# The up layer's second product in two row halves, in a decoder layer on one core

## What is computed

```python
def kmoe(x_flat, W_router, A, B, scale, bias, d_in1, d_in2, d_out1, d_out2, top_k):
    logits = x_flat @ W_router.T
    vals, idx = jax.lax.top_k(logits, top_k)
    probs = jax.nn.softmax(vals, axis=-1)
    xs = x_flat.reshape(-1, d_in1, d_in2)
    Y = jnp.einsum('nkoi,nij,nkpj->nkop', A[idx], xs, B[idx])
    out = jnp.einsum('nkop,nk->nop', Y, probs).reshape(-1, d_out1 * d_out2)
    return out * scale + bias
...
x_flat = x.reshape(-1, 32 * 32)
h = kmoe(x_flat, W_up, A_up, B_up, scale_up, bias_up, 32, 32, 64, 64, 2)
h = jax.nn.gelu(h, approximate=False)
y = kmoe(h, W_down, A_down, B_down, scale_down, bias_down, 64, 64, 32, 32, 2)
```

## Time and profile before

| | us |
|---|---|
| median of three runs | 2138.79 |
| fastest, slowest run | 2125.09, 2139.24 |
| span of the profiled execution | 2129.4 |
| TensorE busy in it | 1763.4 (83%) |
| second product of the up layer, TensorE busy | 170.2 |
| VectorE, ScalarE, GpSimd busy | 975.1, 862.5, 669.1 |

### The profile page before, as it was taken

One profiled execution on the slowest core, in us unless ns is written; L12 is line 12 of the kernel. 1 busy time (PEld: TensorE's weight loads), 2 busy tenths in 40 slices (PEclk: granted clock), 3 DMA queues, 4 the chain that ended last, 5 costly groups with the idle time before them and its releaser, 6 DMA issues.

```text
span 2129.4 us, 54205 instructions
## 1 busy us (share of the span) xinstructions
PE 1763.4 (83%) x17202; PEld 1370.1 (64%) x17202; DVE 975.1 (46%) x3954; ACT 862.5 (41%) x2550; POOL 669.1 (31%) x2386
## 2 busy tenths in 40 slices
PE   6888889798897988879788897988979889797865
PEld 5666757576575665757567575766757657576644
DVE  2345354544535445354443545445354453544543
ACT  2444344343443444345343443434434344343422
POOL 3114242322423134242332423224231242323333
PEclk9998979798797988969899797987979879798977
DMA  7000000000000000000000000000000000000000
GB/s 229 11 6 6 12 1 7 12 7 13 6 2 12 7 12 6 8 7 7 12 6 13 1 7 12 6 13 1 7 12 6 13 6 2 12 2 7 2 6 7
DMA packets 18653, 28.05 MB, mean 13 GB/s; under 512 B 2194, under 2 KB 17171, under 8 KB 18067
## 3 DMA queue, kind: packets, MB, share of 16 engines
q1 hardware_dynamic: 18322, 23.98, 3.7%
HBM read 19.78 MB, written 4.19 MB: 11 GB/s over the span
## 4 chain that ended last, share of the span: by engine, by line
PE 65%; issue 12%; DVE 9%; POOL 7%; POOLq 2%; ACT 2%; DVEq 0%; ACTq 0%
PE P L672 6%; PE G L800 6%; PE P L684 6%; PE G L838 5%; PE P L705 4%; PE X L749 4%; PE G L871 3%; POOL chosen_up L333 3%; PE PT L726 3%; PE P L657 3%; PE X L767 3%; PE PT L767 3%; PE X L752 3%; PE X L751 3%; PE F L824 3%
## 5 line engine op out<-in xcount | busy, mean ns | idle before, releaser
L346 POOL COPY chosen_dn<-experts 64x64 f32 x1024 | 197.1, 250 | 592.5 <-issue 513.1
L333 POOL COPY chosen_up<-experts 32x128 f32 x1024 | 285.6, 303 | 251.8 <-PE G L838 106.9
L970 DVE CUSTOM_DVE_ANT_0 probs<-S,distance 128x128 f32<-128x128 f32 (+1 forms) x512 | 153.5, 354 | 137.5 <-PE S L720 134.8
L557 ACT ACTIVATE probs<-probs,neg_max 128x128 f32<-128x128 f32 (+1 forms) x512 | 190.7, 443 | 41.0 <-DVE neg_max L970 39.7
L749 PE MATMUL X<-vals,probsT 128*128 128x65 f32 x512 | 109.6, 298 | 93.4 <-issue 47.7
L333 ACT COPY chosen_up<-experts 32x128 f32 x512 | 123.1, 292 | 132.8 <-PE G L838 122.7
L838 PE MATMUL G<-chosen_up,W 128*64 128x256 f32 x1024 | 170.2, 462 | 6.9 <-DVE W L1076 6.9
L749 PEld LDWEIGHTS X<-vals,probsT 128*128 128x128 f32 x512 | 83.2, 204 | 124.8 <-issue 123.7
L824 PE MATMUL F<-chosen_up,own 64*64 64x128 f32 x1024 | 98.1, 317 | 68.8 <-POOL chosen_up L333 66.3
L529 ACT ACTIVATE kT<-P,bk 128x256 f32<-128x256 f32 x128 | 53.7, 470 | 233.9 <-PE P L672 233.9
L672 PE MATMUL P<-ctxT,wk 128*128 128x256 f32 x512 | 144.8, 432 | 0.0
(11 more groups left out here) (129 smaller groups left out, 3313.6 us busy)
## 6 DMA issues: line engine op xcount, KB each, us to landing
x<-in_x SPq DMA_DIRECT2D x16, 256.0 KB, 2.6
ctxT<-in_ctxT SPq DMA_DIRECT2D x16, 256.0 KB, 2.6
out<-x2b SPq DMA_DIRECT2D x16, 256.0 KB, 2.9
r_dn<-in_r_dn SPq DMA_DIRECT2D x1, 2048.0 KB, 15.3
experts<-in_experts_up SPq DMA_DIRECT2D x2, 1024.0 KB, 22.0
wk<-in_xWk SPq DMA_DIRECT2D x1, 1024.0 KB
wo<-in_xWo SPq DMA_DIRECT2D x1, 1024.0 KB
wv<-in_xWv SPq DMA_DIRECT2D x1, 1024.0 KB, 7.6
```

What stands on the lines that cost most here:

```text
L333: last = copy(dst, src.rearrange("p (m c) -> p m c", m=2))
L346: last = copy(dst, src.rearrange("p (m c) -> p m c", m=2))
L557: act.activation(probs[e % 4][:, lo:hi], probs[e % 4][:, lo:hi], ACT.Exp, bias=neg_max[:, e % 4, rt:rt + 1], scale=-1.0).then_inc(probs_re ...
L970: dve.tensor_tensor_reduce(probs[e % 4][:, lo:hi], S[e % 2][:, lo:hi], distance[:, (1 - rt) * P:2 * P], SLOPES[e], TOP, ALU.add, ALU.min, ...
```

## The change

The second product is cut along its rows. Rows 0 to 63 hold the first two tokens of a group and rows 64 to 127 the other two, and each half of a block-diagonal matrix has only half of its columns filled. In the new kernel each half is a product of its own, over 64 rows and 128 moving columns: for each k there are four products (row half by group) where there were two. The upper half of the rows goes to bank F, the lower half to bank G, both in columns 256 to 383. The buffers `chosen_up` hold 128 columns for each k in place of 256. `pre` reads both banks in one instruction through a common tensor `FG` and writes the same 256 columns of `h`; the bias table is as wide as one half. Since F is now also read by `pre`, `first(v)` waits for `pre(v-1)` (`hidden_in`) in place of `weigh(v-1)`. `second` keeps its waits, with `hold` for one of them.

```diff
+        HALF = UP_TOK // 2 * F1
...
-        bias_up = sb("bias_up", [P, F1])
+        bias_up = sb("bias_up", [P, HALF])
...
-        A_UP, B_UP = TOPK * UP_TOK * F1, TOPK * F1
+        A_UP, B_UP = TOPK * HALF, TOPK * F1
...
+        FG = ctx.enter_context(nc.psum_tensor("FG", [P, 2, 512], F32))
+        F, G = FG[:, 0, :], FG[:, 1, :]
...
-                a, b = (k * UP_TOK + n) * F1, A_UP + k * F1
+                a, b = k * HALF + n % 2 * F1, A_UP + k * F1
...
-                    pe.wait_ge(W_ready, at(c, TURNS, v))
+                    pe.wait_ge(hidden_in, at(c, UP_PAIRS, v))
...
             def second(c, v):
                 pe.wait_ge(W_ready, at(c, TURNS, v + 1))
                 if v > 0:
-                    pe.wait_ge(hidden_in, at(c, UP_PAIRS, v))
+                    hold(pe, passed, hidden_in, at(c, UP_PAIRS, v))
                 else:
-                    pe.wait_ge(pm_ready, at(c, 6, 4))
-                n = UP_TOK * F1
+                    hold(pe, passed, pm_ready, at(c, 6, 4))
                 for k in range(TOPK):
-                    for j in (0, 1):
-                        w = j * B_UP + k * F1
-                        mm = pe.matmul(G[j * F1:(j + 1) * F1, 0:n], W[v % 2][:, w:w + F1],
-                                       chosen_up[(2 * v + j) % UP_SLOTS][:, k * n:(k + 1) * n], start=(k == 0), stop=(k == TOPK - 1))
+                    for half, to in enumerate((F, G)):
+                        rows = slice(half * F1, (half + 1) * F1)
+                        for j in (0, 1):
+                            w = j * B_UP + k * F1
+                            mm = pe.matmul(to[j * F1:(j + 1) * F1, 256:256 + HALF], W[v % 2][rows, w:w + F1],
+                                           chosen_up[(2 * v + j) % UP_SLOTS][rows, k * HALF:(k + 1) * HALF],
+                                           start=(k == 0), stop=(k == TOPK - 1))
                 mm.then_inc(second_done, 1)
...
-                dve.scalar_tensor_tensor(h[:, v * n:(v + 1) * n].rearrange("p (n o) -> p n o", o=F1),
-                                         G[:, 0:n].rearrange("p (n o) -> p n o", o=F1),
-                                         scale_up[:, 0:1], spread(bias_up[:, :], 1, UP_TOK),
+                dve.scalar_tensor_tensor(h[:, v * n:(v + 1) * n].rearrange("p (t w) -> p t w", t=2),
+                                         FG[:, :, 256:256 + HALF], scale_up[:, 0:1], spread(bias_up[:, :], 1, 2),
                                          ALU.mult, ALU.add).then_inc(hidden_in, 1)
...
-        "bias_up": np.tile(a["L0_ffn_bias_up"].reshape(F1, F1).T, (2, 1)),
+        "bias_up": np.tile(a["L0_ffn_bias_up"].reshape(F1, F1).T, (2, UP_TOK // 2)),
```

More of the change, by code:

```diff
@@ L249, in bank @@
             return ctx.enter_context(nc.psum_tensor(name, [P, 512], F32))
-        S0, S1, PT, X, P0, P1, F, G = (bank(n) for n in ("S0", "S1", "PT", "X", "P0", "P1", "F", "G"))
+        S0, S1, PT, X, P0, P1 = (bank(n) for n in ("S0", "S1", "PT", "X", "P0", "P1"))
+        FG = ctx.enter_context(nc.psum_tensor("FG", [P, 2, 512], F32))
+        F, G = FG[:, 0, :], FG[:, 1, :]
         S = [S0, S1]
```

## The result

The changed kernel takes 2165.61 us (median; 2162.05 to 2174.24), the kernel before, run beside it, 2139.01. The ratio is 1.0167, with an interval of 1.0111 to 1.0223: slower by 1.7%. The forecast was 2121, 0.8% faster, and the result lies above the range that went with it (2093 to 2152).

A forecast was written before the change was run, and what follows sets the result against it. TensorE, busy 83% of the span, was taken as the bound. Over fourteen batches, 21.8 us gained in odd turns less 4.2 for the moved wait gave span 2111.8; with 9.4 us up to the median, 2121 us (range 2093 to 2152).

The forecast's parts named there:

- an odd turn counts: Turns 1, 3, 5, 7: TensorE runs through, so a shorter second brings all behind it earlier, 0.39 us each (0.32 to 0.43).
- the price of the step: TensorE's slot for second: from 1.01 us to 0.62 (bounds 0.58 and 0.69), with four quarters of the array running together.
- The rival of the queue's order: In second: strict program order makes sixteen instructions nine steps, 1.12 us; 2149 us with the wait; chance 0.17.
- the four steps that the prediction set against it: Old second: strict order would need five steps, 1.14 us; the trace has 1.01, about four, so that order seemed not to hold.
- the moved wait in the body: Even turns: first(v+1) waits for pre(v), delaying pv; 0.05 + 0.20 + 0.05 = 0.3 us a batch (0.11 to 0.57).
- I price the odd turns at the high clock all the same: Odd turns: some 36 turns run low, but work pulled from the low stretch draws other work in, so 0.39 us each.
- the chance of the clock: Whole run: chance 0.19 that the granted clock takes the gain, 0.07 of it slower by over 1%.
- The rival of the clock: Behind turns 2 and 4: idle time brings low-clock spells of 1.7 us cost; 28 more give 2169 us; chance 0.19.
- the last two batches, at most 3.1 us of gain: Batches without all three stages: gain of at most 2 x 4 x 0.39 = 3.1 us, left to the range.
- the price of the wait over 14 batches alone: Moved wait counted only in the fourteen full batches: 14 x 0.3 = 4.2 us lost.
- that cover: Even turns of full batches: TensorE's idle time (1.26 and 0.78 us) covers first(v+1)'s wait and is just about used up.
- The range's upper end: 2152 us: strict queue order with the moved wait at its bound, 2138.8 + 6.2 + 8.0 = 2153, rounded in.

The follow-up runs named there:

- e8: Kernel before with four quarter products in odd turns only, plus unread products filling TensorE's idle time in six places of a batch: 2056.60 us, ratio 0.9634.
- e9: Kernel before with exactly the unread filling products of e8, and second unchanged: 2096.14 us, ratio 0.9814.
- e5: Changed kernel plus unread products in TensorE's idle time in turns 2, 4, 6 and ahead of pv of the sixth pair: 2103.59 us, ratio 0.9845.
- e2: Kernel before with the second expert's products left out of second; no moved wait, no 64 x 64 tiles: 2155.81 us, ratio 1.0107.
- e4: Kernel before with four quarter products in odd turns only; first waits for pre only behind an odd turn: 2148.58 us, ratio 1.0072.
- e10: e4 plus two unread products for each batch, ahead of pv of the sixth pair of heads: 2120.97 us, ratio 0.9942.
- e3: Changed kernel with the products of second done twice in even turns: 2147.62 us, ratio 1.0067.
- e1: Kernel before with the changed kernel's waits alone (first(v+1) waits for pre(v)); second keeps 256 columns: 2147.69 us, ratio 1.0079.
- e6: Kernel before plus unread products: two in turn 2, one in turn 4, two ahead of pv of the sixth pair: 2118.37 us, ratio 0.9930.

## Why the prediction was wrong, by its own steps

**Right: an odd turn counts.** From `second` to `score` in turn 7, where neither kernel is at the low clock, it took 3.92 us before (1105.94 to 1109.86 in the rows of before above) and takes 3.50 after (1515.10 to 1518.60), so this odd turn gives 0.42 where 0.39 was forecast; for all of them the 23.4 us between e8 and e9 are the nearest measure.

**Right: the price of the step.** The slot is 0.60 us (0.62 forecast, bounds 0.58 and 0.69). Four instructions start in one step. An instant of the timeline:

```profile
1487.49 0.34 PE L842 MATMUL FG<-chosen_up,W 64*64 64x128 f32 x4
```

Four are in flight at the start, where the earlier trace rows had two. The rival of the queue's order is thus out: nine steps would have taken 1.12 us. The Trainium skill, "TensorE: Matmul & The Clock Gate", Part 3 (packing small matmuls), says that matmuls keep strict program order at start and end. If the two instructions of a product stand side by side, as the prediction took it, the 0.60 us do not bear that out; but no row shows in which order they were issued, so the rule is neither confirmed nor refuted here, nor by the four steps that the prediction set against it.

**Right: the moved wait in the body.** From `second(4)` to `second(5)` it is 4.57 us (1501.91 to 1506.48) against 4.37 before (1092.53 to 1096.90), so 0.20, as forecast (0.11 to 0.35). Turn 2 is 0.09 longer in e5, at the high clock (1442.38 to 1447.33, 4.95, against 4.86 in the earlier trace rows). Turn 6 is 0.11 shorter (3.94 against 4.05), where 0.05 longer was forecast. Together 0.18 a batch instead of 0.3, read from one batch of each kernel.

**Wrong, and the step that failed: "I price the odd turns at the high clock all the same", and the chance of the clock.** By the steps so far a batch should be 4 x 0.41 - 0.18 = 1.5 us shorter. The thirteen batches were 17.1 us longer. The sentence on the earlier trace rows took the low stretches as given and let work only move into or out of them. They are not given: they are set off by how TensorE's work and idle time lie, and shortening the changed step altered where they stand and how long they last. e2 shows it with no other part of the change, e4 with odd turns alone, e5 and e10 in the other direction.

The sizes fit on the whole. Between 14 and 60 us behind `second(0)`, from turn 2 to past `pv` of the sixth pair, the low stretches of the traces add up, over the thirteen batches, to 45 us before, 113 in after, 107 in e2, 79 in e3, 86 in e4 and 0.1 in e5. An estimate takes half of the difference to before and the steps measured above: 0.41 us less for an odd turn (0.43 in e2, whose `second` takes 0.58) and 0.18 more a batch for the wait in after, e3 and e5. It gives the thirteen batches as 15 us longer in after (measured 17.1 longer), 2 shorter in e3 (3.4), 1 shorter in e4 (1.0) and 41 shorter in e5 (39.7). It is no exact price: in e1, e2, e6 and e10 it is off by 5 to 9 us, most in e2 (8 longer, measured 17.1). And low time elsewhere in the batch costs less, for there TensorE also waits: e8 has 68 us more of it than e9 and is shorter all the same.

The rival of the clock had the mechanism and nearly the size (28 more low stretches, 2169 us, against 2165.61). That it came so near is in part luck: it put them behind turns 2 and 4, where after has them behind turn 2 (in 11 of 14 batches, before in 8), behind turn 4 (3, before none) and at `pv` of the sixth pair (10, before 5), and it had nothing for the last two batches. It got a chance of 0.19, with a slow outcome at 0.07, because the rows showed idle time without a fall (0.78 us in turn 4) and the other direction seemed as open. What spoke for it was in the rows and was weighed too lightly: a fall directly behind idle time in the earlier trace rows, two batches 6.2 us apart with the same work, and a mean clock of 0.89 and 0.85 there, which is 22 and 30% of the time at the low level. In turns 2, 4 and 6 the change could only make the idle time longer, by the forecast's own reading, and a longer idle time had no way to a gain.

The Trainium skill, the same page, section "HAM oscillation", describes a loop in which waits between bursts of matmuls bring the clock down in each pass. After agrees in kind, with low stretches behind 1.70 and 1.42 us of idle time. The page's waits are for DMA and longer than these. That an idle time decides by itself is not borne out here: 1.42 us in before were followed by 1.00.

**Wrong: the last two batches, at most 3.1 us of gain, and the price of the wait over 14 batches alone.** I bounded this stage on the side of the gain only. Without attention and Fourier products between the turns, `first(v+1)` had been running under `pre(v)`, and that cover, which I named for even turns of the full batches, goes in every turn. In e1 the last two batches cost 18.6 us, in after, whose `second` is shorter, 11.7. In e2, with a short `second` and no moved wait, they cost 4.8; if after's clock costs as much, an estimate, some 7 of the 11.7 are the wait's. The range's upper end held 8.0 us for the wait, all of it in fourteen batches.

**The sum.** The forecast span was 2111.8, measured were 2163.9, 52.1 more. By parts: 33.4 in the thirteen batches (17.1 longer instead of 13 x 1.26 = 16.3 shorter), 6.0 in the fourteenth (4.7 instead of -1.3), 11.7 in the last two, 1.0 ahead. The first is what the low stretches cost by the estimate above (half of 113 less 45, 34). In the fourteenth batch the clock went from 0.88 to 0.83, and half of the low time that this adds is some 7 us, about the second. In the last two batches wait and clock are mixed. A small term was misread as well: the 9.4 us between span and median are no constant. After's profiled execution took 2165.65 us at a span of 2163.9, so 1.8 us lie around it, and if it is as much in before, the rest was that before's profiled execution was faster than the median one.

**Open.** Why the same idle time is followed by a fall in 12 of 14 batches of e4 and in 5 of 14 of before. A `second(7)` shorter by 0.41 us stands in front of it in e4, but before falls too at times with its long one. The runs show that the fall depends on more than the idle time just ahead of it, and that no fall came there where it was filled (e5, e6 and e10); what the chip goes by they do not show.

## What to carry to other kernels

Where TensorE's granted clock is below 1 for part of the span, cost a change by what it does to the idle time in front of and behind each TensorE step, not by the step alone: shortening work in front of a wait lengthens the wait, and here that turned a forecast gain of 0.8% into a loss of 1.7%. Before such a change is judged, fill the idle time with a few products that nobody reads, in both kernels; here that gave 1.9% without the change and 3.7% with the part of it that counts. And when a wait is moved, look at the stages in which the other work is missing, for there the cover is missing too.

## What was not expected of the hardware

- Doing more made it faster: two unread products for each batch, ahead of one `pv`, took 28 us off e4 (2148.58 to 2120.97; by the ratios 1.3%).
- Leaving out half of a step's work (e2) made the kernel 1.1% slower, with the low time at 668 us instead of 545.
- Sixteen instructions on four quarters of the array held TensorE for 0.60 us, eight on two quarters 0.58: the doubled number cost 0.02.
